# Turning the image to pixel order inside the drain of the feed-forward part, half a pair of images at a time, with ScalarE and VectorE applying the norm factor as the blocks leave PSUM

## The reference, cut to what matters

```python
x = x + _L0_conv_ref(_gn(x), ...)    # windowed attention + feed-forward, 32 images of 64 channels x 32 x 32
x = x + _L1_conv_ref(_gn(x), ...)    # block scoring, top 6 of 64 pixels per block, a small MLP
return x

def _gn(v, G=32, eps=1e-05):         # v is (B, H, W, C): here (32, 64, 32, 32), so a group is
    g = v.reshape(B_, H_, W_, G, C_ // G)      # one column w, taken over the 64 channels and 32 rows
    m = jnp.mean(g, axis=(1, 2, 4), keepdims=True)
    s = jnp.var(g, axis=(1, 2, 4), keepdims=True)
    return ((g - m) / jnp.sqrt(s + eps)).reshape(v.shape)

# in _L1_conv_ref: 16 blocks of 8 x 8 pixels per image
scores = jnp.einsum('gbcl,gc->gbl', xb, conv_w)
e = jnp.exp(scores); p = e / jnp.sum(e, axis=-1, keepdims=True)
_, idx = jax.lax.top_k(p, K)          # K = 6
```

## Time and profile before

| | |
|---|---|
| median of 3 runs | 830.89 us (830.06 to 833.17) |
| the profiled execution's own time | 831.67 us |
| its span, first to last instruction | 829.9 us |
| mean granted TensorE clock | 0.898 of full speed |
| TensorE busy | 699.6 us |
| VectorE busy | 516.4 us |
| ScalarE busy | 488.6 us |
| GpSimd busy | 374.4 us |

### The profile page before, as it was taken

How to read it: one execution, slowest core, us unless ns; L and a number is a source line. 1 busy time by engine, 2 the same in 40 slices (tenths; PEclk the granted TensorE clock), 3 DMA queues, 4 the chain that set the end, 5 groups by cost and what they waited for, 6 DMA issues and landing times. The chain is left out here.

```text
span 829.9 us, 21353 instructions
## 1 busy us (share of the span) xinstructions
PE 699.6 (84%) x8482; PEld 371.9 (45%) x8482; DVE 516.4 (62%) x964; ACT 488.6 (59%) x986; POOL 374.4 (45%) x464
## 2 busy tenths in 40 slices
PE   4774799999999999999998569999999757929870
PEld 3562355555555555555554223333333226826340
DVE  4791367777766667777768211677777875772171
ACT  3663367777777777777775448877777305825000
POOL 4696255777676776777676420011222234400000
PEclk9775599999999999999999959999999857959955
DMA  9630000000000000000000020012122213000167
GB/s 216 147 87 11 1 2 2 2 2 2 2 2 3 2 3 2 3 2 3 3 2 2 2 52 1 25 51 53 52 51 52 52 26 98 0 0 2 47 187 261
DMA packets 15719, 31.41 MB, mean 38 GB/s; under 512 B 7489, under 2 KB 9285, under 8 KB 15621
## 3 DMA queue, kind: packets, MB, share of 16 engines
q1 hardware_dynamic: 12592, 29.16, 13.2%
q10 hardware_dynamic: 2760, 0.66, 0.5%
q0 software_dynamic: 272, 0.27, 0.2%
HBM read 20.71 MB, written 9.37 MB: 36 GB/s over the span
## 5 line engine op out<-in xcount | busy, mean ns | idle before, releaser
L757 POOL TENSOR_TENSOR sc<-sc,mx 128x512 f32<-128x512 f32 x128 | 133.8, 1045 | 34.2 <-DVE mx L705 34.2
L702 DVE TENSOR_TENSOR sc<-s_ps,bias_tab 128x512 f32<-128x512 f32 x128 | 87.7, 685 | 59.1 <-PE s_ps L532 59.1
L655 ACT ACTIVATE pt<-t_ps 128x512 f32<-128x512 f32 x128 | 76.0, 594 | 52.6 <-PE t_ps L543 51.4
L1199 POOL TENSOR_TENSOR square<-xs 128x1024 f32<-128x1024 f32 x16 | 33.8, 2112 | 162.1 <-DVE xs L1101 162.1
L705 DVE TENSOR_REDUCE mx<-sc 128x8 f32<-128x512 f32 x128 | 87.8, 686 | 4.4
L1018 ACT ACTIVATE hs<-h_ps,fb1s 128x512 f32<-128x512 f32 x128 | 78.2, 689 | 17.7 <-PE h_ps L932 17.6
L543 PEld LDWEIGHTS t_ps<-consts,sc 128*128 128x128 f32 x512 | 53.7, 141 | 73.1 <-issue 45.9
L543 PE MATMUL t_ps<-consts,sc 128*128 128x128 f32 x512 | 83.9, 286 | 2.2 <-ACT pt L655 1.6
L532 PE MATMUL s_ps<-kx,qu 32*64 32x128 f32 x2048 | 71.5, 276 | 1.5 <-DVE sc L702 1.4
L932 PE MATMUL h_ps<-xs,fw 64*128 64x512 f32 x256 | 68.5, 649 | 1.0 <-ACT hs L1018 1.0
L945 PE MATMUL c_ps<-hs,fw 128*64 128x512 f32 x256 | 62.0, 604 | 0.8 <-DVE fcsq L1045 0.7
(11 more groups left out here) (190 smaller groups left out, 1360.0 us busy)
## 6 DMA issues: line engine op xcount, KB each, us to landing
raw<-in_x_dram SPq DMA_DIRECT2D x32, 256.0 KB, 4.7
xr<-in_x_dram SPq DMA_DIRECT2D x32, 256.0 KB, 4.0
out_dram<-x SPq DMA_DIRECT2D x32, 256.0 KB, 4.1
rec_scratch<-r SPq DMA_DIRECT2D x4, 224.0 KB, 2.5
w<-in_L_conv_W_dram SPq DMA_DIRECT2D x1, 784.0 KB
w<-in_L_conv_W_dram SPq DMA_DIRECT2D x1, 672.0 KB
xs<-rec_scratch SPq DMA_DIRECT2D x16, 28.0 KB
xs<-rec_scratch ACTq DMA_DIRECT2D x16, 28.0 KB
```

The costliest lines, as they stand in the source:

```text
L655: act.activation(pt[a][2 * hp + j][:, :, :], t_ps[:, :, :], ACT.Exp).then_inc(s["exped"], 1)
L702: dve.tensor_tensor(sc[n % KEPT][:, :, :, :], s_ps[j][:, :, :, :], bias_tab[:, j, hp], ALU.add)\
L757: pool.tensor_tensor(v, v, mx[n % KEPT][:, :].unsqueeze(2).broadcast_to([128, 8, TOK]), ALU.subtract)\
```

## The change

The turn stage is gone as a stage. Its work is done inside the forward stage's block:

- `centre` writes `xs[:, p]` in block order, with four instructions of 256 elements in the place of one of 1024.
- The square sums of even and odd block columns go to separate columns of `n_ps`, and `fold_square` reduces 256 elements in the place of 128.
- No multiplication with the factor comes before the turning. The factor of a pixel is the same for all channels of an image, so it is applied after turning, when pixels are partitions, as one number per partition. For that, the variance of each image column (`turn_var`), its Ln and Exp (`turn_rstds` on 32 partitions), a spreading to pixel partitions (`spread_pixels`) and a copy make `pixel_rstd`, in two batches: pairs 0 to 9 and pairs 10 to 15.
- Turning is cut into 32 jobs of half a pair (4 block pairs, 4 matmuls of 132 columns). `turn` now holds per image 64 columns of the identity and two of `conv_w`, so a job's result is in the layout of `yt`, whose blocks have 66 columns per image.
- `take_turned` on ScalarE empties a job with 4 activations of 132 elements, each with a per-partition scale. `multiply_turned` on VectorE empties a job with 2 multiplications of 264 elements.
- Jobs 0 to 19 (pairs 0 to 9) use two places of two banks each, of which the hidden matmuls were the users before, and are all emptied by ScalarE. Jobs 20 to 31 use three places, and VectorE (even) and ScalarE (odd) take turns.
- TensorE's drain is a new hand-written list, `tensor_drain`: 16 jobs are placed among the steps of the drain, 16 follow its last square sum, with the second batch's factor after job 20.
- The loads for the tail (L1325) and the clearing of `ow`, `st_t` and `r` go into the tail stage; `iota` is loaded in the forward stage.

```diff
@@ layout and banks
+        LEAD = 512
+        flat = sb(whole, "xs", [128, LEAD + PAIRS * PIX])
+        xs = flat[:, LEAD:].rearrange("c (p n) -> c p n", p=PAIRS)
...
+        yt = flat[:, 0:PAIRS * 8 * TURN].rearrange("c (p g a n) -> c p g a n", p=PAIRS, g=8, a=2)
...
@@ pair_square_sum
-                    sum_rows(pe, square[:, k]).then_inc(s["sq_ps"], 1)
+                    for e in range(2):
+                        for g in range(4):
+                            at = 128 * (2 * g + e)
+                            last = pe.matmul(n_ps[rows(g), 128 * e:128 * (e + 1)], group_rows, square[:, k, at:at + 128],
+                                             start=True, stop=True)
+                    last.then_inc(s["sq_ps"], 1)
@@ centre, fold_square
-                    dve.tensor_tensor(xs[:, p].rearrange("c (h w) -> c h w", w=W),
...
+                    for y in range(4):
+                        last = dve.tensor_tensor(xs[:, p].rearrange("c (y x h w) -> c y x h w", y=4, x=4, h=WS)[:, y],
+                                                 x1[:, p].rearrange("c (y h x w) -> c y x h w", y=4, h=WS, x=4)[:, y],
+                                                 mean, ALU.subtract)
...
-                    fold(dve, sqsums[:, p]).then_inc(s["sqsum"], 1)
+                    dve.tensor_reduce(sqsums[:, p].rearrange("c (x w) -> c x w", x=4),
+                                      n_ps[:, 0:256].rearrange("c (x h w) -> c x w h", x=4, h=WS), X, ALU.add)\
+                       .then_inc(s["sqsum"], 1)
@@ new
+            def turn_job(pe, j):
+                p, half = j // 2, j % 2
+                pe.wait_ge(s["centred"], p + 1)
+                if j == 0:
+                    pe.wait_ge(s["zero"], 5)
+                if j < 2:
+                    pe.wait_ge(s["gelu"], 4 * UNITS)
+                elif turn_place(j) == 2 and j < 2 * EARLY + 3:
+                    pe.wait_ge(s["scaled"], UNITS)
+                else:
+                    taken(pe, max(i for i in range(j) if turn_place(i) == turn_place(j)))
+                for n in range(4):
+                    gp = 4 * half + n
+                    last = pe.matmul(TURN_BANKS[turn_place(j)][:, n // 2, TURN * (n % 2):TURN * (n % 2 + 1)],
+                                     xs[:, p, 128 * gp:128 * (gp + 1)], turn[:, gp], start=True, stop=True)
+                last.then_inc(s["turned"], 1)
...
+            def take_turned(act, j):
+                act.wait_ge(s["pixel_rstd"], 1 if j < 2 * EARLY else 2)
+                act.wait_ge(s["turned"], j + 1)
+                for e in range(2):
+                    for a in range(2):
+                        last = act.activation(turn_blocks(j, e)[:, :, a], turn_fill(j)[:, :, e, a], ACT.Copy,
+                                              scale=pixel_rstd[:, e, j // 2, a:a + 1])
+                last.then_inc(s["turn_a"], 1)
+
+            def multiply_turned(dve, j):
+                dve.wait_ge(s["pixel_rstd"], 2)
+                dve.wait_ge(s["turned"], j + 1)
+                for e in range(2):
+                    factor = pixel_rstd[:, e, j // 2].unsqueeze(1).unsqueeze(3).broadcast_to([128, 2, 2, SIDE])
+                    last = dve.tensor_tensor(turn_blocks(j, e), turn_fill(j)[:, :, e], factor, ALU.mult)
+                last.then_inc(s["turn_b"], 1)
...
+            def tensor_drain(pe):
...
+                pair_mean(pe, 5, 1)
+                output(pe, 7, 3)
+                pair_square_sum(pe, 5, 0)
+                spread_rstd(pe, 6, 1)
+                turn_jobs(1)
+                variances(pe, 7)
+                turn_var(pe, 0)
+                turn_jobs(1)
+                pair_sum(pe, 6, 0)
+                spread_rstd(pe, 7, 0)
+                spread_pixels(pe, 0)
+                pair_mean(pe, 6, 0)
+                turn_jobs(1)
+                pair_square_sum(pe, 5, 1)
+                turn_jobs(2)
+                pair_sum(pe, 6, 1)
...
+                pair_mean(pe, 7, 1)
+                turn_jobs(1)
+                pair_square_sum(pe, 7, 0)
+                turn_jobs(1)
+                pair_square_sum(pe, 7, 1)
+                turn_jobs(2 * EARLY + 1 - 16)
+                turn_var(pe, 1)
+                turn_jobs(1)
+                spread_pixels(pe, 1)
+                turn_jobs(JOBS - 2 * EARLY - 2)
...
@@ scalar and vector streams, after their steps
+                    turn_rstds(act, 0)
+                    for j in range(2 * EARLY):
+                        take_turned(act, j)
+                    turn_rstds(act, 1)
+                    for j in range(2 * EARLY + 1, JOBS, 2):
+                        take_turned(act, j)
...
+                    for j in range(2 * EARLY, JOBS, 2):
+                        multiply_turned(dve, j)
@@ turn stage: removed whole (variance, Ln, Exp, scale, turn, copies, its loads and memsets)
@@ tail stage
+                @block.gpsimd
+                def _(pool):
+                    pool.memset(ow[:, :], 0.0).then_inc(tail_zero, 1)
+                    pool.memset(st_t[:, :, :], 0.0)
+                    for t in range(2):
+                        last = pool.memset(r[:, t], 0.0)
+                    last.then_inc(tail_zero, 1)
...
-                        last = dve.tensor_copy(scores[lo:hi], raw_scores[lo:hi, :, :, 2 * b:2 * b + 2])
+                        last = dve.tensor_copy(scores[lo:hi], yt[lo:hi, :, :, :, C + b])
```

More of the change, by code:

```diff
@@ new lines, in build, with turn_place, turn_by_act, taken @@
+            TURN_BANKS = [h_all[:, 0:2], h_all[:, 2:4], r_all[:, 0:2]]
+            def turn_place(j):
+                return j % 2 if j < 2 * EARLY else j % 3
+            def turn_by_act(j):
+                return j < 2 * EARLY or j % 2 == 1
+            def taken(eng, j):
+                if turn_by_act(j):
+                    eng.wait_ge(s["turn_a"], sum(turn_by_act(i) for i in range(j + 1)))
+                else:
+                    eng.wait_ge(s["turn_b"], sum(not turn_by_act(i) for i in range(j + 1)))
@@ new lines, in turn_fill, with turn_blocks, turn_var @@
+            def turn_fill(j):
+                return TURN_BANKS[turn_place(j)][:, :, 0:2 * TURN].rearrange("c y (e a n) -> c y e a n", e=2, a=2)
+            def turn_blocks(j, e):
+                return yt[:, j // 2].rearrange("c (h y e) a n -> c h y e a n", h=2, e=2)[:, j % 2, :, e]
+            def turn_var(pe, b):
+                first, last_pair = BATCHES[b]
+                pe.wait_ge(s["sqsum"], last_pair)
+                if b == 0:
+                    pe.wait_ge(s["out"], UNITS)
+                    pe.wait_ge(s["csq"], UNITS)
+                else:
+                    pe.wait_ge(s["pixel_rstd"], b)
+                for p in range(first, last_pair):
+                    last = pe.matmul(c_ps[0:W, 2 * p:2 * p + 2], sqsums[:, p], spread_image[:, 0:128:C], start=True, stop=True)
+                last.then_inc(s["turn_var"], 1)
@@ new lines, in turn_rstds @@
+            def turn_rstds(act, b):
+                first, last_pair = BATCHES[b]
+                at = slice(2 * first, 2 * last_pair)
+                act.wait_ge(s["turn_var"], b + 1)
+                act.activation(turn_rstd[:, at], c_ps[0:W, at], ACT.Ln, bias=eps[0:W, 0:1]).then_inc(s["turn_rstd"], 1)
+                act.wait_ge(s["turn_rstd"], 2 * b + 1)
+                act.activation(turn_rstd[:, at], turn_rstd[:, at], ACT.Exp, scale=-0.5).then_inc(s["turn_rstd"], 1)
+                act.wait_ge(s["pixel_ps"], b + 1)
+                act.activation(pixel_rstd[:, :, first:last_pair].rearrange("c e p a -> c e (p a)"),
+                               c_ps[:, 64:192].rearrange("c (e n) -> c e n", e=2)[:, :, at], ACT.Copy)\
+                   .then_inc(s["pixel_rstd"], 1)
@@ L1255, in build @@
         ow = sb(whole, "ow", [128, 128])
-        iota = sb(whole, "iota", [128, TOK])
         PICKS = 32
```

179 lines of the change are left out of this document (78 added, 101 removed).

## The result

The changed kernel takes 811.08 us (median of 4 runs, 809.35 to 812.75), the kernel before 831.78 in the same comparison: ratio 0.9755, 95% interval 0.9734 to 0.9775, so 20.4 us faster by the ratio. The forecast was 812.9 with a range of 807 to 820. The profiled execution of the changed kernel took 809.35 us, with a span of 807.4 and a mean granted clock of 0.930 (0.898 before).

A forecast was written before the change was run, and what follows sets the result against it. TensorE sets the steady steps; VectorE the drain, with TensorE half idle, and turning follows. Drain +1.6 and +1.0, after its last square sum -21.6, tail +1.0: -18.0 on 831.67 gives 813.7, median 812.9, range 807 to 820.

The forecast's parts named there:

- Step 1: Steady steps: longer centring (+0.25 a pair) and fold (+0.13) on VectorE, costed at zero as hidden by TensorE's full step.
- rival C: Steady steps: VectorE's longer centre and fold not hidden, +4.6 us, 817.5; chance 0.20 shared with the memset rival.
- Steps 2 and 3: Drain: VectorE's longer centres and folds +1.6 us; 16 jobs at full clock, delays equal to gains, +1.0 for misfits.
- Step 5: After the last square sum: jobs 16 to 20 5.8, factor 2.2, jobs 22 to 31 11.0, last take and barrier; 20.5 us.
- behind D: From the end of the last square sum's matmuls to the tail: 20.5 us against 42.1, so -21.6.
- Step 4: ScalarE in the drain: a take costs 1.16 us a job, jobs 0 to 19 need 23 us, not the limit there.
- Step 6: Tail: loads hidden; memsets beside the chain of picks and strided score copies cost +1.0 us together, memset bounds 0 and 3.6.
- rival D: Tail: the chain of picks is caught by both memsets, 3.6 for 1.0 us, 815.5; chance 0.20 shared with the steady-step rival.
- The sum: Whole kernel: drain +1.6 and +1.0, after the last square sum -21.6, tail +1.0, together -18.0 us.
- Its signs: Expected in the trace: no barrier, clock near 1.0, jobs 1.05, takes 1.16, last square sum 687 to 689, tail 708 to 710.
- Rival A: Drain: TensorE stays at half clock until its end, 14.4 us late there, 824.6; chance 0.10 in part, 0.03 in full.
- Rivals B and E: B: half clock until the tail, 836, chance 0.04. E: drain misfits zero, clock gains more than jobs delay, 809, chance 0.13.

The follow-up runs named there:

- e1: Changed kernel with all 32 turning jobs placed behind the drain's last square sum; ratio 1.0022 to the kernel before.
- e2: Kernel before with only the four-instruction block-order centring, square sums in two column ranges and folds of 256 elements; ratio 1.0048.
- e3: Changed kernel with ScalarE's takes as plain copies, norm factor left out; one profiled execution, no ratio, 0.9 us less between last square sum and score copies.
- g3: Changed kernel with the 1.8 us memset of the first half of r as GpSimd's first tail work; score copies 2.32 us, picks 1.5 later.
- e4: Changed kernel with GpSimd's larger tail memsets held until the scores are copied; the two score copies take 0.80 us against 1.00.
- e5: Changed kernel with three places and both engines emptying from job 16 on, second batch's variance behind job 16, larger tail memsets held back; ratio 0.9745.
- f1: Changed kernel with all mends: moved column sum, three places and both engines emptying from job 16 on, late memsets; 809.42 us, ratio 0.9719.
- f2: Changed kernel with the second pair's column sum moved behind the next step's first hidden half; ratio 0.9750.

## Why the prediction was right, point by point

- *The aim and the sign* were right, and by the named mechanism: the jobs fill the drain, which VectorE still sets (9.66 and 9.81 busy), and e1 gives all of it back.
- *Step 1, VectorE in the steady steps, "I cost it at zero; TensorE's full step hides it": this failed.* It costs 0.33 us a step, 1.4 in all, 30% of the 4.6 that rival C had. The working read room from VectorE's busy share (15.82 of 21.5) where it had to ask for each added instruction who waits for it. The fold stands directly ahead of a sum on a full TensorE. The sizes of the instructions were right: 0.20 for the centring and 0.13 for the fold, against 0.25 and 0.13.
- *Steps 2 and 3, the drain, +2.6*: measured +0.7 in the profile of the changed kernel, and +2.3 in the four with the fall of the clock (42.8 against 40.51). The working took full clock for granted and had no term for its coming and going, which is worth 1.6. What VectorE's extras of 1.6 cost by themselves can't be read off: e2 has +0.6 with part of the clock kept, e1 +2.6 with the clock lost and the factor's small matmuls in it. Where the clock stayed, it gave back more than the jobs' delays cost, so the +1.0 for misfits was too much there.
- *Step 5, behind D, 20.5 us*: 18.77. Jobs 16 to 20 took 5.6 (5.8 said), the factor and its waits 2.1 (2.2), jobs 22 to 31 9.6 (11.0), last take and barrier 1.5 (1.5). The mis-sized term is a job at 1.05: that was the old loop's pace with its waits for ScalarE's copies in it (TensorE was busy 4.33 of 5 us there, 0.91 of the 1.05), not TensorE's price. TensorE alone needs 0.90.
- *Step 4, a take at 1.16 us*: measured 1.16. But as the pace of jobs 16 to 20 it left out the refill: 1.27.
- *Step 6, the tail, +1.0*: +0.2 for the picks, within what this distance varies by, and as little to the end (102.1 us from the score copies on, 101.95 before). The two copies are 0.4 us longer, half by what I take for the stride and half by a memset, and most of that is under ScalarE's table load, as the step says. The bounds of 0 and 3.6 were fair. The mechanism of rival D is real, but what it catches are the score copies: 1.8 us in e3, which has the changed kernel's order of memsets, and 1.5 in g3. The changed kernel escapes it by 0.4 us of timing.
- *The sum* was -18.0 and is -21.1 by the distances. An error of +1.4 (the steps) stands against -1.9 (the drain), -1.8 (behind D) and -0.8 (the tail). The forecast of 812.9 against 811.1 is better than its parts, and this is in part luck: it also has the kernel before 0.9 us lower (830.89) than it came out in the comparison (831.78).
- *Its signs*: no barrier, the clock and the take of 1.16 came as said. The last square sum (686.5, not 687 to 689), the tail's start (705.3, not 708 to 710) and the job (0.90, not 1.05) came out lower. The sign against it for rival C, a step longer than 21.5 us, showed.
- *Rival A in part*: the clock's fall for 3 to 4 us, 1.6 us a time, in four of six profiles with the gap of 1.24 us. *Rivals B and E* didn't come; E's condition (the clock gains more than the jobs delay) did where the clock stayed, in smaller size.

## What to carry to other kernels

Idle time of an engine beside a bound one can be filled with work from a later stage, and filling half of it already gave 12 of the 22 us. What a filling costs there depends on the clock: with half of it a job took up to 2.1 us of TensorE, not 1.17, and that drain was the longest. So price the work at full clock only if the filling is dense enough that a profile shows that clock. Before an added instruction is called hidden, look for the wait that it stands ahead of, not at the busy share of its engine; a full pipeline can have no room in a place where nothing waits yet. And a loop's pace is no price of one engine's work, while its waits are in it.

## What the runs showed of the hardware beyond what was expected

- The same instruction lists with the same gap of 1.24 us kept full clock in two profiled executions (the changed kernel, e4) and lost it for 3 to 4 us in two (e5, g3); with one sum moved it was lost in both (f1, f2). The drain is 41.2 or 42.8 us by it, with nothing in between in these six.
- The steady stage repeats to 0.02 us across kernels with the same list (150.40 to 150.42 in seven profiles of one list), while its start moves by up to 3.3 us (487.66 to 490.98 for the first Gelus of kernels that are the same up to there). Such a distance inside one trace resolves what five times of a kernel (intervals of 1.5 to 2.6 us to either side) can't.
- A VectorE copy of 0.39 us that starts 0.04 us behind a GpSimd memset of 1.8 us ends only 0.15 us after it, though the two share no data (g3).
- The same copy with no memset beside it takes 0.39 us reading every 66th element, and 0.29 from the old layout (e4, before).
- Breaking a run of eight matmuls that use 64 of the 128 rows by others costs about 0.2 us of TensorE (1.92 against 2 x 1.06, f2).

What stays open: what decides whether the clock falls in the same list with the same gap (the gap of 0.88 us and the filled one were seen once each); why the first score copy of e3 lost to a memset that it beat elsewhere; and whether the mends beat the changed kernel outright; the distances say 1.8 us, the times don't separate them.
